# A bf16 matmul that nothing reads, behind the steps of two recurrences of 256 steps

## The reference, cut to what matters

```python
def step(state, u_t):
    state = jnp.tanh(state @ A.T + u_t)
    return (state, state)
_, states = jax.lax.scan(step, init, u_tm)
```

## Time and profile before

| what | us |
|---|---|
| median of 3 runs | 778.38 (778.14 to 780.07) |
| span of the profiled execution, first to last instruction | 775.8 |
| TensorE busy (matmuls) in the span | 566.2 |
| VectorE busy | 340.6 |
| ScalarE busy | 336.1 |
| first recurrence, 26 to 162 us of the span | 136.0 |
| second recurrence, 368.8 to 518.5 us | 149.7 |

### The profile page before, as it was taken

One profiled execution on the slowest core, in us unless ns is written; L12 is line 12 of the kernel. 1 busy time (PEld: TensorE's weight loads), 2 busy tenths in 40 slices (PEclk: granted clock), 3 DMA queues, 4 the chain that ended last, 5 costly groups with the idle time before them and its releaser, 6 DMA issues. The chain is left out here.

```text
span 775.8 us, 10987 instructions
## 1 busy us (share of the span) xinstructions
PE 566.2 (73%) x4080; PEld 324.7 (42%) x4081; DVE 340.6 (44%) x734; ACT 336.1 (43%) x1095; POOL 0.2 (0%) x4
## 2 busy tenths in 40 slices
PE   6665566567877999986566666665899998995463
PEld 5322222235645766664333333333455544551321
DVE  2170000049757788875200000006887546776233
ACT  2233333337737677772333333334544465442121
POOL 0000000000000000000000000000000000000000
PEclk9755555559997999997555555558999999997577
DMA  4000000000000000000000000004000000000000
GB/s 166 1 1 1 1 0 1 1 0 1 3 0 1 2 1 2 2 1 1 1 1 1 0 1 1 0 1 108 1 2 1 1 1 1 2 1 0 8 5 27
DMA packets 4954, 6.73 MB, mean 9 GB/s; under 512 B 1186, under 2 KB 4642, under 8 KB 4772
## 3 DMA queue, kind: packets, MB, share of 16 engines
q1 hardware_dynamic: 4900, 6.01, 2.5%
HBM read 3.38 MB, written 0.52 MB: 5 GB/s over the span
## 5 line engine op out<-in xcount | busy, mean ns | idle before, releaser
L303 PE MATMUL ps<-arena,wsb 16*16 16x16 f32 (+1 forms) x1024 | 131.5, 206 | 111.1 <-ACT arena L321 111.1
L321 ACT ACTIVATE arena<-ps 16x16 f32<-16x16 f32 (+1 forms) x512 | 96.3, 188 | 199.3 <-PE ps L303 199.3
L303 PEld LDWEIGHTS ps<-arena,wsb 16*16 16x16 f32 (+1 forms) x1024 | 76.4, 118 | 196.2 <-ACT arena L321 191.7
L327 DVE TENSOR_TENSOR X<-X,ps 128x128 f32<-128x128 f32 x16 | 4.6, 288 | 206.6 <-PE ps L288 206.6
L965 ACT ACTIVATE arena<-ps 128x512 f32<-128x512 f32 x96 | 56.6, 597 | 62.0 <-PE ps L726 60.7
L1267 DVE TENSOR_TENSOR arena<-arena,ps 128x512 f32<-128x512 f32 x96 | 64.0, 685 | 41.2 <-ACT arena L965 24.9
L744 PE MATMUL ps<-arena 128*32 128x128 f32 x768 | 60.3, 279 | 7.3 <-DVE arena L1267 7.3
L889 ACT ACTIVATE arena<-ps,arena 128x128 f32<-128x128 f32 (+1 forms) x128 | 52.4, 418 | 29.9 <-DVE arena L1140 29.8
L744 PEld LDWEIGHTS ps<-arena 128*32 128x32 f32 x768 | 34.8, 109 | 41.9 <-DVE arena L1267 22.6
L1139 DVE TENSOR_REDUCE arena<-ps 128x2 f32<-128x512 f32 (+1 forms) x48 | 33.0, 688 | 18.6 <-PE ps L569 11.1
L586 PE MATMUL ps<-wsb,arena 128*128 128x128 f32 x192 | 30.4, 282 | 11.6 <-DVE arena L1148 11.5
(11 more groups left out here) (231 smaller groups left out, 805.8 us busy)
## 6 DMA issues: line engine op xcount, KB each, us to landing
arena<-xn SPq DMA_DIRECT2D x16, 128.0 KB, 2.5
wsb<-weights SPq DMA_DIRECT2D x1, 1916.5 KB, 8.8
wsb<-weights SPq DMA_DIRECT2D x1, 549.5 KB, 4.8
X<-x SPq DMA_DIRECT2D x1, 512.0 KB, 3.9
out<-X SPq DMA_DIRECT2D x1, 512.0 KB, 3.0
csb<-consts SPq DMA_DIRECT2D x1, 160.0 KB, 8.8
arena<-w SPq DMA_DIRECT2D x2, 64.0 KB
arena<-b SPq DMA_DIRECT2D x4, 0.5 KB
```

The source lines that it names most:

```text
L303: nc.tensor.matmul(step_columns(k, rows, r), w_state, states[0:rows, :, :, t].rearrange("p g j -> p (g j)"), start=False, stop=True, skip_ ...
L321: nc.scalar.activation(states[0:rows, :, :, t + 1].rearrange("p g j -> p (g j)"), step_columns(t // STEP_BANK, rows, t % STEP_BANK), func) ...
```

## The change

Behind a step's matmul, TensorE gets one more: the bf16 identity times 384 columns of `csb` (zeros and two masks), with 128 rows and 128 columns of the array in use, into the bank two ahead of the one being stepped. Nothing reads the result; a fill with `start=True` overwrites it later. It is left out behind the steps 4, 7, 10, 13, 17, 20, 23 and 26 of each bank, in all banks alike. That makes 24 x 8 = 192 in each recurrence, 384 in all. Waits are added so that a bank is not written before its last reader is done: at the start of some banks TensorE waits for "L0 skip added", "F input" or "bank added", a new semaphore that VectorE raises with each `add_bank_out`. The two waits that stood at a fill go away, and the normalisation after the second recurrence waits for "bank added" in place of "X ready".

```diff
+SPARE_COLS = 384
+SPARE_NOT_AT = (4, 7, 10, 13, 17, 20, 23, 26)
...
+        by_spare = csb[:, CCOL["zeros"][0]:NC]
...
-                pe.wait_ge(s["X ready"], n + 1)
+                pe.wait_ge(s["bank added"] if n == 3 else s["X ready"], 2 * BANKS if n == 3 else n + 1 - (n > 3))
...
+        def spare_matmul(k):
+            nc.tensor.matmul(ps[:, (k + 2) % BANKS, 0:SPARE_COLS], CB("identb"), by_spare[:, 0:SPARE_COLS], start=True, stop=True)
+
         def recur_tensor(pe, n, rows, w_in, w_state, w_out):
+            pe.wait_ge(s["consts loaded"], 16)
             for t in range(T):
                 k, r = t // STEP_BANK, t % STEP_BANK
                 if r == 0 and n == 0:
                     pe.wait_ge(s["bank biased"], k + 1)
+                if r == 0 and k + 2 == (6 if n == 0 else 4):
+                    pe.wait_ge(s["L0 skip added" if n == 0 else "F input"], 2)
+                if r == 0 and k >= BANKS - 2:
+                    pe.wait_ge(s["bank added"], BANKS * n + k + 3 - BANKS)
                 if t > 0:
                     pe.wait_ge(s["state"], n * T + t)
                 nc.tensor.matmul(step_columns(k, rows, r), w_state, states[0:rows, :, :, t].rearrange("p g j -> p (g j)"),
                                  start=False, stop=True, skip_group_check=True).then_inc(s["pre-state"], 1)
+                if r not in SPARE_NOT_AT:
+                    spare_matmul(k)
                 if k > 0 and r in (4, 7, 10, 13):
                     bank_out(k - 1, (r - 4) // 3, rows, w_out)
                 if k < BANKS - 1 and r in (17, 20, 23, 26):
-                    if n == 0 and k + 1 == 6 and r == 17:
-
-                        pe.wait_ge(s["L0 skip added"], 2)
-                    if n == 1 and STEP_BANK * (k + 1) == P and r == 17:
-                        pe.wait_ge(s["F input"], 2)
                     bank_fill(n, k + 1, (r - 17) // 3, rows, w_in)
...
-            return nc.vector.tensor_tensor(cols, cols, ps[:, k, 0:P].rearrange("p (j t) -> p j t", j=J), ALU.add)
+            return nc.vector.tensor_tensor(cols, cols, ps[:, k, 0:P].rearrange("p (j t) -> p j t", j=J), ALU.add)\
+                .then_inc(s["bank added"], 1)
...
-            link(add_bank_out(dve, 0, BANKS - 1))
+            add_bank_out(dve, 0, BANKS - 1)
+            dve.wait_ge(s["bank added"], BANKS)
...
             for k in range(BANKS):
-                ins = add_bank_out(dve, 1, k)
-            ins.then_inc(s["X ready"], 1)
+                add_bank_out(dve, 1, k)
```

More of the change, by code:

```diff
@@ L457, in _ @@
             routed("sync", sp, attention, feed_forward)
-            sp.wait_ge(s["X ready"], 6)
+            sp.wait_ge(s["X ready"], 5)
             sp.dma_start(out.rearrange("(j g) c h w -> (g c) j (h w)", g=G), Xj).then_inc(s["stored"], 16)
```

## The result

| | before | after |
|---|---|---|
| median of 4 runs, us | 778.75 (778.14 to 780.07) | 812.76 (807.65 to 814.47) |
| profiled execution, own time and span | | 814.47, 812.7 |
| TensorE busy, us | 566.2 | 711.1 |
| first recurrence, first to last ScalarE step | 135.5 | 150.7 |
| second recurrence, the same | 149.2 | 165.6 |

The ratio is 1.0435, with a 95% interval of 1.0389 to 1.048: slower by 34 us, where 26 us less were forecast. The profiled execution is the slowest of the four; its span is 36.9 us longer than that of before. Its own time lies 1.8 us above its span.

What follows compares the result with a forecast made beforehand. Each recurrence was taken as one chain of latencies, TensorE and ScalarE waiting on each other. -7.4 - 19.1 + 1.6 + 0.5 - 1.8 = -26.2 gave span 749.6, median 752.2 us; range 746 to 780, the forecast's own 747 to 760.

Steps and rivals of the forecast that it cites:

- The step that failed: Both recurrences: the added full-array bf16 matmuls were taken as likelier to bring TensorE's granted clock to full than leave it half.
- The row from 639.8 on: Earlier trace, a later 3.4 us stretch: three 128x512 bf16 matmuls, 1.87 us busy, clock stayed 1.00; taken as nearest to the change.
- Rival B: In the 384 steps the clock stays at half, each 0.11 us longer, 42 us in all, giving 821; chance 0.14.
- Added matmul at full clock, free: Behind a step: 384 columns take 0.33 us, next step may start at 0.41, not ready before 0.50; no cost.
- First recurrence at full clock, 128.6: First recurrence: 256 steps of 0.50 us, fills hidden, bank starts 0.6; 128.6 against 136.0, so -7.4 us.
- VectorE's cover: First recurrence: VectorE's bias of bank 2 ends near 56.7, step 64 comes at 58.2; free, 1.5 us of cover.
- Second recurrence at full clock, 0.51 a step: Second recurrence: 256 steps of 0.51 us, 130.6 against 149.7, so -19.1 us (bounds -21.7 to -6).
- Start of the second recurrence: It begins at half clock; about ten steps cost 0.67 us, not 0.51, until the clock rises: +1.6 (0 to +6).
- Waits at a bank's start, +0.5: Banks 4, 6, 7 of the first and 2, 6, 7 of the second recurrence: one more wait, 0.08 us each.
- After the recurrences, -1.8: Centring behind the second recurrence runs at full clock, 1.98 us in place of 3.78: -1.8 (0 to -1.8).
- Rival D: Full clock, but the added matmul's weight load holds up the next step by 0.02 us: +8, so 760; chance 0.12.
- Rival C: The clock comes and goes, at half for a third of the steps where added matmuls are missing: 775; chance 0.12.

Runs made afterwards that it cites:

- e7: The changed kernel with an fp32 matmul of 96 columns in place of the bf16 one of 384: 900.63 us beside 777.61 for the kernel before.
- e3: The changed kernel with random weights and operands in the added matmul in place of identity, zeros and masks: 812.51 us beside 775.86 before.
- e11: e10 with 384 added columns behind its steps in place of 512: 840.87 us beside 775.53 for the kernel before.
- e10: e8 plus 512-column bursts, eight matmuls ahead of the second recurrence, ten behind the first; four double steps, not eight: 755.08 us beside 775.04 before, ratio 0.9747.
- e6: The changed kernel with 512 columns, full-array fills and outputs, and two added matmuls behind the second recurrence's first 8 steps: 883.32 us beside 777.61 before.
- e8: e6 with 512 added columns also behind the bare steps of the first and last bank: 830.89 us beside 776.82 for the kernel before.
- e12: e10 with the narrow fills and outputs of the change in place of full-array ones: 835.5 us beside 775.53 for the kernel before.
- e9: e8's work in the second recurrence alone, the first as before the change: 835.47 us beside 776.82 for the kernel before.
- e4: The changed kernel with two added matmuls of 512 columns behind every step, none left out: 879.22 us beside 775.86 for the kernel before.
- e1: The changed kernel with 256 added columns in place of 384: 775.43 us beside 775.86 for the kernel before.
- e2: The changed kernel with 384 columns, but the added matmul only on the step's 16 or 32 rows and columns: 778.61 us beside 775.86 before.

## Why the prediction was wrong

**The step that failed** is that on the clock: "By kind that is the first row and not the second, so I take full clock as the likelier". One row that stayed at 1.00 with thin bf16 work, and one that fell behind fp32 work, were read as a rule by kind. In its place the runs show the bf16 work over the full array at 0.50 in both recurrences, but for the first 6.7 us, and e7 and e3 leave neither the kind nor the values as the cause. What told the kernels apart, once the clock was up, is how much each step streams over the full array, and whether any step is thin: 384 columns fell where 512 held (e11 against e10), three bare steps in the first bank were enough for a fall (e6 against e8), and so were a few outputs of 16 or 32 rows (e12 against e10). The row from 639.8 on could not carry the conclusion: e11 too stood at 1.00 from 21.1 to 27.3 and from 397.5 to 402.8, and then at 0.50 for the rest of each recurrence. The nearest row in kind of work was the recurrence itself: filled with fills and outputs, at 0.50.

Rival B is what happened, in kind and place, and its argument, that work between the steps had never lifted the clock, was the better one. Its price was high: 0.11 us for each against 0.087, or 42 us in all where the recurrences grew by 31.6, since the matmul took 0.50 us at half clock and not the 0.53 taken between two greatest values, each of them perhaps a record across a change. It gave 821; the median is 812.76.

The other steps, in order:

- *Added matmul at full clock, free.* Right: 0.50 us a step up to 32.7 us, with a matmul of 0.34 (0.33 forecast). Even 512 columns cost nothing there (e8, e10).
- *First recurrence at full clock, 128.6.* Not seen with narrow fills for longer than the start, but its terms stood: 0.50 a plain step, hidden fills (e12), bank starts of 0.584 (e8, e10). With full-array fills it took 132.3 (e10). VectorE's cover was enough there too, with banks starting on time.
- *Second recurrence at full clock, 0.51 a step.* 0.515 (e10). The fills' gain holds with narrow fills (e12).
- *Start of the second recurrence.* The term took for granted that a matmul behind each step lifts the clock within some steps. In e8 and e9 even 512 columns did not do it in 206 us; in e4 and e6, with two such matmuls behind each of the first steps, it rose 1.2 us after the start.
- *Waits at a bank's start, +0.5.* Nothing in the kernel of the change: 0.594 and 0.647 us there as elsewhere, since the added matmul covers them. Where it leaves room, the three of the second recurrence cost 0.07 us each (0.627 for 0.560 in e1, 0.585 for 0.515 in e10), near the price of 0.08, and the three of the first, which already wait for "bank biased", nothing.
- *After the recurrences, -1.8.* It did not come: the centring (L233) took 3.78 us again, at half clock as in the earlier trace rows. It hung on the clock. In e10 that stretch ran at 1.00 (493.3 to 498.0).
- *Rival D* did not occur: no plain step of the first recurrence over 0.50 us at full clock, and 0.515 in the second, bare or not (e6). *Rival C* came half true in e6 and e12: the clock fell at the thin places, but it did not rise again in the fuller ones.

By the Trainium skill, "TensorE: Matmul & The Clock Gate", section "What's actually happening", activity releases the throttle. If activity is what the profile calls busy, the trace of the change disagrees, with 0.50 throughout 166.5 us in which TensorE was busy 99% of the time, and so does e8, at 100%.

**What stays open** is which quantity the chip follows, and when half clock is left. In e4 and e6 the clock fell some 2.2 us ahead of the second recurrence and rose 1.2 us after its start. In e8 and e9, which have e6's fills ahead and its two matmuls of 512 columns behind each of the first eight steps, it fell 2.9 and 2.8 us ahead and did not rise. Stretches of e6, up to the rise and behind it, then the first eight steps of e8:

```profile
421.10:424.50 3.40, 3.40 (x15) 2.22 (x16) 2.48 (x5) 0.26 (x2) 0.00 (x0) 0.50 0.01 2
424.50:431.30 6.80, 5.97 (x36) 2.29 (x34) 3.60 (x8) 2.19 (x12) 0.00 (x0) 1.00 0.01 2
...
361.70:371.20 9.50, 9.50 (x33) 2.44 (x33) 4.80 (x8) 1.55 (x9) 0.00 (x0) 0.50 0.01 2
```

So the work of the steps alone does not tell whether the clock rises, and no run tells what does. Nor does the number of columns explain every stretch: that from 639.8 on the earlier trace rows stayed at 1.00 with three full-array matmuls of 512 columns in 3.4 us, fewer full-array columns than e11 streams in such a time. No width between 384 and 512 columns was tried.

## What to carry to other kernels

Filling TensorE's gaps is no way to a faster clock by itself: a filler that does not hold the clock runs at half rate, and then lengthens the chain that it was to hide in. Try the filler that surely holds it first (a double one, as e4), then read from the granted clock at what thin place it falls; pauses ahead of the stretch count too (e8 against e10). And before buying a clock, price the chain at both levels from single steps: here full clock was worth 3 us in one recurrence and 13 in the other, while half clock put 0.09 us on every filled step.

## What the runs showed that I had not expected

- A busy TensorE is not enough. It was busy 206.60 of 206.60 us at 0.50 (e8), and 132.87 of 133.20 at 1.00 (e10).
- A matmul began 0.07 us behind a step with the same 16 rows (e2), but 0.16 us behind it when it used all 128 (the change). By the Trainium skill, the same page, section "The mechanism", a weight load overlaps a running matmul only where the row groups differ. The trace of e2 disagrees: the weight load for the step's own rows began at 100.01, while the step's matmul ran (99.97 to 100.20, both records of it together).
- The step hardly feels the clock: 0.500 us at full and 0.507 at half with 16 rows, 0.515 and 0.560 with 32. What feels it is what stands between the steps: a fill costs 0.19 to 0.22 us at half clock and nothing at full.
- 96 fp32 columns took 0.74 us behind a step at half clock, 384 bf16 columns 0.50 (e7).
